# Sampling stage of a deformable bottleneck: transposes dealt three at a time, one table load and two DVE/ACT orders moved

## The chip, the cores and the metric

The kernel runs on one core of one Trainium2 chip. The metric is device time in microseconds (us), as the median of several runs. A core has five instruction queues that run side by side and meet at semaphores: TensorE (PE, matrix multiplies and transposes into PSUM), VectorE (DVE), ScalarE (ACT, activations and copies), GpSimd (POOL) and SyncE (SP, which issues the DMAs here). Each queue works through its own program in order.

## The reference

Two bottleneck blocks follow each other on x of 4 images x 256 channels x 16 x 16. The first is a deformable convolution block, the second a convolution block with quantised weights and activations:

```
out = relu(group_norm(conv1x1(x, w1)))                  # 256 -> 64 channels
om  = conv3x3(out, w_off) + b_off                       # 27 channels: x and y offsets, mask of 9 taps
sampled = bilinear_sample(out, grid_y + off_y, grid_x + off_x) * sigmoid(mask)
out = einsum('bckhw,ock->bohw', sampled, w2)            # 9 taps
out = relu(group_norm(out))
out = relu(group_norm(conv1x1(out, w3)) + x)            # 64 -> 256 channels
# second block: quantise -> conv1x1 -> depthwise 3x3 -> bn, relu -> conv3x3 -> bn, relu -> conv1x1 -> bn -> + residual, relu
```

## The kernel before, in words

The four images are held as `HALVES` = 2 by `B2` = 2. The change lies in the sampling stage, which does the bilinear sampling as matrix products. For each tile t (b2 = t // 2, and t % 2 is one half of the image's 256 output pixels) and half h there is one **unit** i = 2t + h, eight in all.

- **Hats.** DVE takes the differences of positions and coordinates (`differences`, L849), makes them into hat functions, and `apply_mask` (L863) multiplies one of the two by the mask. For tiles 2 and 3 ACT does the hat part (`distance`, L653, two activations).
- **g rows.** `make_g` (L874) on DVE is the product of the two hats, one 16 x 16 image of weights per output pixel and tap, into one of three buffers `g_rows`. Units 0 to 5 are made whole; the last two units (6 and 7) are made in thirds of three taps. `make_g` of unit i waits until the turns of unit i - 3 are done.
- **Turns.** `turn(n)` (L433) on PE transposes a third of a unit (12 PE transposes) into one of three PSUM slots. It waits for the unit's g rows and for the copy of turn n - 3, which frees its slot. There are 24 turns (n = 0 to 23). Turns 18 to 23 are, in this order, thirds of units 6, 7, 6, 7, 6, 7.
- **Copies.** `copy_g(n)` (L686) on ACT moves the slot of turn n to SBUF (`g_cols`). Between copies ACT does other work that is placed by n: `distance`, Sign, Abs and Identity of the second block's weights, and `root` and `normalise` of the second group norm of b2 = 0.
- **Samples.** `sample(t, a, b)` (L453) on PE multiplies taps a to b of tile t with the features (`v_sb`) and adds into `acc[b2]`; 4 matmuls a tap, of which the trace shows 8 records. It waits for the copies of the two turns that hold the tap.
- **Means.** `sample(1, 8, 8)` ends b2 = 0 and raises `sampled`; DVE's `moments(0)` then lets PE's `pair_sums(3, 0)` run, after which DVE's `pair_var`, ACT's `root(3, 0)` (behind copy 18), DVE's `pair_scale` and ACT's `normalise` (behind copy 19) make `feat2` for `conv3(0)` (L497), which starts the next stage. `conv3(0)` waits for `feat2` and for all 24 copies.

The order of turns and samples on PE is written out by hand (L466 to L494). `idle(n, bank)` (L336) are n matmuls on zeros that compute nothing. Ahead of the stage, ACT copies `v_sb` out of PSUM (`copy_v`, L663), the last of them at L681, and then loads the table of Sqrt (L696) before `copy_g(0)`; the table of Sigmoid was loaded at L670 for the masks.

Of the kernel before, what the change touches and what calls it, by code (L numbers as in the profile page):

```python
# [51 lines left out]
ROWS_Q = H // NQ  # L52
PER_SLOT = 3
SLOT_OF = (1, 2, 0)
IDLE_FIRST = 2
TURNS = TAPS // PER_SLOT

TAPS_A = 5
# [6 lines left out]
WHOLE = UNITS - HALVES  # L65
# [26 lines left out]
ACT = mybir.ActivationFunctionType  # L92
# [20 lines left out]
def build(nc, x, first, pairs, consts, woff, grid, w2, w3, wq, out):  # L113
    with ExitStack() as ctx:
# [6 lines left out]
        def sem(name):  # L121
            return ctx.enter_context(nc.semaphore(name))
# [116 lines left out]
        diff_ready = sem("diff_ready")  # L239
# [9 lines left out]
        sampled = sem("sampled")  # L249
# [85 lines left out]
        def _(pe):  # L335
# [97 lines left out]
            def turn(n):  # L433

                i, j = THIRDS[n]
                pe.wait_ge(g_ready, products_before(i, j))
                if n < TURNS:

                    pe.wait_ge(v_ready, (1, 6, 2 * T + 1)[n])
                else:  # L440

                    pe.wait_ge(g_copied, n - TURNS + 1)
                for k in range(PER_SLOT * j, PER_SLOT * j + PER_SLOT):
                    for q in range(NQ):
                        at = CB * (NQ * (k - PER_SLOT * j) + q)
                        for r in range(HALVES):
                            mm = nc.tensor.transpose(  # L447
                                slot[SLOT_OF[n % TURNS]][:, BANK * r + at:BANK * r + at + CB],
                                g_rows[i % 3][rows(r), k, ROWS_Q * q:ROWS_Q * q + ROWS_Q, :],
                                ident[rows(r), CB * r:CB * r + CB])  # L450
                mm.then_inc(turned, 1)

            def sample(t, first_tap, last_tap):  # L453

                b2, at = t // NQ, P * (t % NQ)
                for k in range(first_tap, last_tap + 1):
                    pe.wait_ge(g_copied, third_after(t, k))
                    for q in range(NQ):
                        for h in range(HALVES):
                            mm = nc.tensor.matmul(  # L460
                                acc[b2][rows(h), at:at + P], v_sb[:, B2 * h + b2, q, k, :],
                                g_cols[t][h][:, NQ * k + q, :],
                                start=(k == 0 and q == 0), stop=(k == TAPS - 1 and q == NQ - 1))
                return mm

            for n in range(2 * TURNS):  # L466
                turn(n)
            idle(IDLE_FIRST, acc[1][:])

            sample(0, 0, 2)  # L470
            for n, first_tap, last_tap in ((6, 3, 3), (7, 4, 4), (8, 5, 5), (9, 6, 6), (10, 7, 7), (11, 8, 8)):
                turn(n)
                sample(0, first_tap, last_tap)
            sample(1, 0, 2)
            for n, first_tap, last_tap in ((12, 3, 3), (13, 4, 4), (14, 5, 5), (15, 6, 6), (16, 7, 7)):
                turn(n)
                sample(1, first_tap, last_tap)
            turn(17)
            sample(1, 8, 8).then_inc(sampled, 1)
            sample(2, 0, 0)  # L480
            turn(18)
            sample(2, 1, 2)
            turn(19)
            pair_sums(3, 0)
            sample(2, 3, 3)
            turn(20)
            sample(2, 4, 5)
            turn(21)
            sample(2, 6, 6)
            turn(22)  # L490
            sample(2, 7, 7)
            turn(23)
            sample(2, 8, 8)
            sample(3, 0, 1)  # L494


# [116 lines left out]
        def _(a):  # L613
# [33 lines left out]
            def copy_omt(b2):  # L647
                a.wait_ge(omt_done, b2 + 1)
                nc.scalar.activation(omt_sb[:, b2].rearrange("p q h o -> p (q h o)"),
                                     slot[1][:, BANK * b2:BANK * b2 + NQ * CB], ACT.Copy).then_inc(omt_ready, 1)  # L650
                make_mask(b2)
# [21 lines left out]
            copy_v(0)  # L673
            copy_v(1)
            copy_omt(1)
            for i in range(2, 2 * T):
                copy_v(i)

            a.wait_ge(v_done, 2 * T + 1)
            for h in range(HALVES):  # L680
                last = nc.scalar.activation(v_sb[:, B2 * h:B2 * h + B2, :, V_MAIN, :],  # L681
                                            slot[0][:, BANK * h:BANK * h + T * CB].rearrange(
                                                "p (b q o) -> p b q o", b=B2, q=NQ), ACT.Copy)
# [9 lines left out]
                nc.scalar.activation(dst.rearrange("p k (r n) -> p k r n", r=HALVES),  # L693
                                     src.rearrange("p r (k n) -> p k r n", k=per), ACT.Copy).then_inc(g_copied, 1)

            nc.scalar.preload_act_table(ACT.Sqrt)  # L696
            for n in range(len(THIRDS)):
                copy_g(n)
                if n == 5:
                    distance(2)  # L700
                if n == 8:
                    a.wait_ge(wq_in, 16)
                    nc.scalar.activation(wq_sign[:], wq_sb[:], ACT.Sign).then_inc(sign_ready, 1)
                if n == 11:
                    distance(3)
                if n == 13:
                    nc.scalar.activation(wq_mag[:], wq_sb[:], ACT.Abs).then_inc(sign_ready, 1)
                if n == 16:
                    a.wait_ge(sign_ready, 2)
                    nc.scalar.activation(wq_mag[:], wq_mag[:], ACT.Identity, scale=SQRT2, bias=tiny_sb[:, 0:1]  # L710
                                         ).then_inc(sign_ready, 1)
                if n == 18:
                    root(3, 0)
                if n == 19:
                    normalise(3, 0, feat2[:, 0, :], acc[0][:, 0:N], feat2_ready)
# [64 lines left out]
            for i, (c, b2, h, n) in enumerate(PIECES):  # L780
                a.wait_ge(sum_ready, 4 * B2 + i + 1)
                if i == len(PIECES) - 1:
                    n = 1
# [4 lines left out]
        def _(dve):  # L788
# [23 lines left out]
            def moments(b2):  # L812

                settle(nc.vector.bn_stats(stats[:, b2, 0, :], acc[b2][:, 0:N]))  # L814
                nc.vector.bn_aggr(mv[:, b2, 0, :], stats[:, b2, 0, :]).then_inc(mv_ready, 1)

            def pair_var(done, b2):

                dve.wait_ge(sums_done, done)
                sums = sums_of(done, b2)  # L820
                ts(var[:, b2, 0:1], sums[:, 4:5], sums[:, 4:5], sums[:, 1:2], ALU.mult, ALU.add  # L821
                   ).then_inc(var_ready, 1)
# [26 lines left out]
            def differences(t):  # L849

                dve.wait_ge(omt_ready, t // NQ + 1)
                return tt(hats[:, t].rearrange("p h a k y -> p h (a k) y"),
                          omt_sb[:, t // NQ, t % NQ, :, 0:2 * TAPS].unsqueeze(3).to_broadcast(
                              [P, HALVES, 2 * TAPS, H]),
                          coord.unsqueeze(1).unsqueeze(1).to_broadcast([P, HALVES, 2 * TAPS, H]), ALU.subtract)
# [7 lines left out]
            def apply_mask(t):  # L863

                if t < NQ:
                    dve.wait_ge(hats_made, t + 1)
                else:
                    dve.wait_ge(relu1_ready, t - 1)
                dve.wait_ge(mask_ready, t // NQ + 1)
                tt(hats[:, t, :, 1], hats[:, t, :, 1],  # L870
                   mask[:, t // NQ, t % NQ].unsqueeze(3).to_broadcast([P, HALVES, TAPS, H]), ALU.mult
                   ).then_inc(hats_ready, 1)

            def make_g(i, first_tap=0, last_tap=TAPS - 1):  # L874

                t, h = i // HALVES, i % HALVES
                taps = slice(first_tap, last_tap + 1)
                shape = [P, last_tap + 1 - first_tap, H, W]
                dve.wait_ge(hats_ready, t + 1)
                if i >= 3:  # L880

                    dve.wait_ge(turned, TURNS * (i - 2))
                tt(g_rows[i % 3][:, taps], hats[:, t, h, 1, taps].unsqueeze(3).to_broadcast(shape),  # L883
                   hats[:, t, h, 0, taps].unsqueeze(2).to_broadcast(shape), ALU.mult).then_inc(g_ready, 1)
# [23 lines left out]
            settle(differences(1))  # L908
            make_hats(1)
            apply_mask(1)  # L910
            differences(2).then_inc(diff_ready, 1)
            make_g(2)
            make_g(3)
            apply_mask(2)
            differences(3).then_inc(diff_ready, 1)
            make_g(4)
            make_g(5)
            apply_mask(3)
            for j in range(TURNS):
                for i in (WHOLE, WHOLE + 1):  # L920
                    make_g(i, PER_SLOT * j, PER_SLOT * j + PER_SLOT - 1)
                if j == 0:
                    dve.wait_ge(sampled, 1)
                    moments(0)
                if j == 1:
                    pair_var(3, 0)
                    pair_scale(3, 0, V_GN2S, V_GN2B)

            def eight_moments(b2):
                for c in range(CH):  # L930
# [79 lines left out]
            last = residual(1)  # L1010
# [178 lines left out]
```

## Time and profile before

| | us |
|---|---|
| median of 3 runs | 99.76 (99.13 to 100.64) |
| profiled execution, device time | 99.62 |
| its span (first to last instruction) | 97.8 |
| PE busy / DVE busy / ACT busy | 80.4 / 66.7 / 54.4 |
| start of the span to the first sample | 27.4 |
| first sample to `conv3(0)` | 25.8 |
| `conv3(0)` to the end | 44.6 |

The profile is of one execution. Times inside it are us from the start of the span. A busy engine is not always the one that sets the end: the chain of work that ended last names, at each moment, the instruction that the end was waiting for. "PEclk" is the granted clock of TensorE, as a share of 2.4 GHz.

### The profile page before, as it was taken

To read this page: it belongs to the slowest core of one execution; us is meant where nothing else is said; L and a number is where in the kernel's file an instruction comes from. 1 tells how busy PE (TensorE), PEld (TensorE's weight loads), DVE (VectorE), ACT (ScalarE), POOL (GpSimd) and SP (SyncE) were. 2 spreads that over 40 slices of the span, in tenths; PEclk is the share of its full clock that TensorE was granted. 3 is DMA by queue.
4 is the path that set the end of the run, shared out by engine and by line. 5 is a ranking of instruction groups with operands and counts; after the bars stand their busy time and mean duration, and the time that the engine had idled before them with its cause. 6 is when DMAs were issued, how large, how long until landed. Compare 5 with 4: busy or idle time off the path is not lost.

```text
span 97.8 us, 2194 instructions
## 1 busy us (share of the span) xinstructions
PE 80.4 (82%) x891; PEld 55.1 (56%) x896; DVE 66.7 (68%) x184; ACT 54.4 (56%) x94; POOL 5.0 (5%) x10
## 2 busy tenths in 40 slices
PE   5989998973899999999999997999576949597400
PEld 1335654663678798788878884475132448283100
DVE  1235389999999935309693706595989785857960
ACT  5102566699976897996683005531638064444770
POOL 7401100000000000000004000000000000000000
PEclk9999999999579999999999999999999999999955
DMA  2999500000000000000000000000000000000066
GB/s 34 290 358 314 221 0 0 7 0 0 0 7 0 0 7 0 7 7 0 0 7 0 0 0 7 0 0 0 0 0 0 0 0 0 0 10 0 0 204 225
DMA packets 3274, 4.17 MB, mean 43 GB/s; under 512 B 256, under 2 KB 2688, under 8 KB 3264
## 3 DMA queue, kind: packets, MB, share of 16 engines
q1 hardware_dynamic: 2992, 3.76, 12.0%
q10 hardware_dynamic: 272, 0.26, 0.8%
q8 instruction: 7, 0.11, 0.5%
q14 instruction: 3, 0.02, 0.1%
HBM read 2.98 MB, written 1.05 MB: 41 GB/s over the span
## 4 chain that ended last, share of the span: by engine, by line
PE 56%; DVE 18%; ACT 12%; DMA 5%; issue 3%; SPq 2%; DVEq 0%; ACTq 0%
PE acc L460 19%; PE slot L447 12%; DMA x_sb<-x 5%; PE acc L590 5%; PE slot L501 4%; ACT v_sb L666 3%; DVE g_cols L1015 3%; ACT g_cols L785 3%; PE slot L375 2%; PE acc L339 2%; PE slot L339 2%; ACT pad L754 2%; DVE g_cols L969 1%; DVE unused L987 1%; PE slot L530 1%
## 5 line engine op out<-in xcount | busy, mean ns | idle before, releaser
L883 DVE TENSOR_TENSOR g_rows<-hats 128x2304 f32<-128x2304 f32 (+1 forms) x12 | 20.6, 1752 | 1.1 <-PE slot L447 1.0
L460 PE MATMUL acc<-g_cols,v_sb 128*64 128x128 f32 x288 | 21.0, 284 | 0.0
L693 ACT ACTIVATE g_cols<-slot 128x768 f32<-128x768 f32 x24 | 18.7, 814 | 3.4 <-PE slot L447 3.4
L460 PEld LDWEIGHTS acc<-g_cols,v_sb 128*64 128x64 f32 x288 | 15.7, 139 | 2.4 <-ACT g_cols L693 0.8
L447 PE MATMUL slot<-consts_sb,g_rows 64*128 64x64 f32 x288 | 14.5, 237 | 2.4 <-ACT g_cols L693 1.5
L339 PE MATMUL slot<-zeros 128*128 128x512 bf16 x49 | 14.0, 415 | 1.5 <-DVE zeros L804 1.2
L447 PEld LDWEIGHTS slot<-consts_sb,g_rows 64*128 64x128 f32 x288 | 11.6, 146 | 5.8 <-issue 4.8
L339 PEld LDWEIGHTS slot<-zeros 128*128 128x128 bf16 x53 | 5.2, 107 | 6.8 <-issue 2.5
L754 ACT ACTIVATE pad<-g_cols 64x256 bf16<-64x256 int8 x8 | 3.3, 418 | 4.8 <-DVE g_cols L1015 4.7
L814 DVE BATCH_NORM_STATS2 stats<-acc 128x6 f32<-128x256 f32 x4 | 1.7, 429 | 4.9 <-PE acc L460 2.9
L623 ACT ACTIVATE std<-var,eps_sb 128x1 f32<-128x1 f32 x4 | 1.2, 294 | 6.7 <-DVE var L821 6.7
L375 PE MATMUL slot<-feat,woff_sb 128*64 128x256 f32 x36 | 4.7, 385 | 0.0
L737 ACT ACTIVATE dev_sb<-slot 128x4 f32<-128x4 f32 x2 | 0.3, 174 | 7.5 <-PE slot L511 7.5
L933 DVE BATCH_NORM_STATS2 stats<-slot 128x6 f32<-128x256 f32 x8 | 3.0, 414 | 2.0 <-PE slot L501 2.0
L339 PE MATMUL acc<-zeros 128*128 128x512 bf16 x14 | 3.9, 396 | 0.3 <-issue 0.3
L501 PE MATMUL slot<-feat,w_sb 128*128 128x256 f32 x16 | 4.0, 392 | 0.1
L530 PE MATMUL slot<-consts_sb,mx 128*128 128x128 f32 x12 | 2.4, 282 | 1.8 <-DVE mx L973 1.8
L725 ACT ACTIVATE g_cols<-slot,gn_bias,gn_scale 128x256 f32<-128x256 f32 x6 | 2.9, 560 | 1.4 <-DVE gn_bias L951 1.4
L777 ACT ACTIVATE act<-raw,bn_off 128x256 f32<-128x256 f32 x4 | 2.0, 508 | 2.8 <-DVE mx L1091 2.8
L501 PEld LDWEIGHTS slot<-feat,w_sb 128*128 128x128 f32 x16 | 2.9, 189 | 1.1 <-ACT feat L628 0.6
L870 DVE TENSOR_TENSOR hats<-hats,mask 128x288 f32<-128x288 f32 x4 | 1.8, 452 | 2.4 <-ACT hats L659 2.4
L375 PEld LDWEIGHTS slot<-feat,woff_sb 128*64 128x64 f32 x36 | 2.7, 135 | 1.2
(128 smaller groups left out, 120.8 us busy)
## 6 DMA issues: line engine op xcount, KB each, us to landing
out<-g_cols SPq DMA_DIRECT2D x4, 256.0 KB, 2.3
x_sb<-x SPq DMA_DIRECT2D x3, 256.0 KB, 4.5
wq_sb<-wq SPq DMA_DIRECT2D x1, 484.5 KB, 6.3
woff_sb<-woff SPq DMA_DIRECT2D x1, 288.0 KB, 5.5
w_sb<-w SPq DMA_DIRECT2D x1, 288.0 KB, 5.6
x_sb<-x ACTq DMA_DIRECT2D x1, 256.0 KB, 3.0
w_sb<-w SPq DMA_DIRECT2D x1, 256.0 KB, 6.5
consts_sb<-consts SPq DMA_DIRECT2D x1, 232.0 KB, 5.4
```

What stands on the lines that cost most here:

```text
L339: nc.tensor.matmul(bank, zeros[:, 0:P], zeros[:], start=True, stop=True)
L375: mm = nc.tensor.matmul(slot[0][CB * p:CB * p + CB, BANK * b2:BANK * b2 + N], woff_sb[:, k, :], window(feat, b2, k), start=(s == 0), stop= ...
L447: mm = nc.tensor.transpose(slot[SLOT_OF[n % TURNS]][:, BANK * r + at:BANK * r + at + CB], g_rows[i % 3][rows(r), k, ROWS_Q * q:ROWS_Q * q ...
L460: mm = nc.tensor.matmul(acc[b2][rows(h), at:at + P], v_sb[:, B2 * h + b2, q, k, :], g_cols[t][h][:, NQ * k + q, :], start=(k == 0 and q == ...
L501: mm = nc.tensor.matmul(slot[c][:, BANK * b2 + N * h:BANK * b2 + N * h + N], w3_sb[:, h, P * c:P * c + P], feat2[:, b2, :], start=True, st ...
L530: nc.tensor.matmul(small[b2][:, P:2 * P], mx[:, n, b2:b2 + 1].to_broadcast([P, P]), ident, start=not biased, stop=True, is_transpose=not b ...
L590: mm = nc.tensor.matmul(acc[b2][rows(h), 0:N], weights(k), window(pad[:, b2], h, k), start=(k == 0), stop=(k == TAPS - 1))
L666: nc.scalar.activation(v_sb[:, B2 * h + b2, q, 0:V_MAIN, :].rearrange("p k o -> p (k o)"), v_banks[i % 4], ACT.Copy).then_inc(v_ready, 1)
L693: nc.scalar.activation(dst.rearrange("p k (r n) -> p k r n", r=HALVES), src.rearrange("p r (k n) -> p k r n", k=per), ACT.Copy).then_inc(g ...
L754: nc.scalar.activation(dst, src, ACT.Copy, scale=256.0).then_inc(hi_ready, 1)
L883: tt(g_rows[i % 3][:, taps], hats[:, t, h, 1, taps].unsqueeze(3).to_broadcast(shape), hats[:, t, h, 0, taps].unsqueeze(2).to_broadcast(sha ...
L933: last = nc.vector.bn_stats(stats[:, b2, HALVES * c + h, :], slot[c][:, BANK * b2 + N * h:BANK * b2 + N * h + N])
```

## The change

On PE, turns are dealt three at a time (a whole unit, or three thirds of units 6 and 7) between runs of two to six taps, instead of one turn between runs of mostly one tap. The dummy matmuls ahead of the first sample go from 2 to 3. On ACT, the load of Sqrt's table moves from behind the `v_sb` copies to behind the second mask; `distance(3)` moves from behind copy 11 to behind copy 8 and Sign from behind copy 8 to behind copy 10. On DVE, the differences of tile 2 come behind `make_g(2)` instead of ahead of it, those of tile 3 ahead of `apply_mask(2)`, and the last thirds move around the moments and the variance.

```
-IDLE_FIRST = 2
+IDLE_FIRST = 3
...
+            turns(0, 5)
             idle(IDLE_FIRST, acc[1][:])
-
-            sample(0, 0, 2)
-            for n, first_tap, last_tap in ((6, 3, 3), (7, 4, 4), (8, 5, 5), (9, 6, 6), (10, 7, 7), (11, 8, 8)):
-                turn(n)
-                sample(0, first_tap, last_tap)
...
+            sample(0, 0, 4)
+            turns(6, 8)
+            sample(0, 5, 6)
+            turns(9, 11)
+            sample(0, 7, 8)
+            sample(1, 0, 3)
+            turns(12, 14)
+            sample(1, 4, 6)
+            turns(15, 17)
+            sample(1, 7, 8).then_inc(sampled, 1)
+            sample(2, 0, 3)
+            turns(18, 20)
             pair_sums(3, 0)
...
+            sample(2, 4, 6)
+            turns(21, 23)
+            sample(2, 7, 8)
             sample(3, 0, 1)
...
             copy_omt(1)
+            nc.scalar.preload_act_table(ACT.Sqrt)
             for i in range(2, 2 * T):
                 copy_v(i)
...
-            nc.scalar.preload_act_table(ACT.Sqrt)
             for n in range(len(THIRDS)):
                 copy_g(n)
                 if n == 5:
                     distance(2)
-                if n == 8:
+                if n == 10:
                     a.wait_ge(wq_in, 16)
                     nc.scalar.activation(wq_sign[:], wq_sb[:], ACT.Sign).then_inc(sign_ready, 1)
-                if n == 11:
+                if n == 8:
                     distance(3)
...
+            make_g(2)
             differences(2).then_inc(diff_ready, 1)
-            make_g(2)
             make_g(3)
+            differences(3).then_inc(diff_ready, 1)
             apply_mask(2)
-            differences(3).then_inc(diff_ready, 1)
             make_g(4)
             make_g(5)
             apply_mask(3)
...
+            make_third(0, 0)
+            make_third(0, 1)
+            make_third(1, 0)
+            dve.wait_ge(sampled, 1)
+            moments(0)
+            make_third(1, 1)
+            make_third(2, 0)
+            pair_var(3, 0)
+            pair_scale(3, 0, V_GN2S, V_GN2B)
+            make_third(2, 1)
```

`turns(a, b)` calls `turn` for n = a to b. `make_third(j, h)` makes the third j of unit 6 + h. Before, the order was (0,0), (0,1), moments, (1,0), (1,1), variance and scale, (2,0), (2,1).

On PE, from the first sample on, L447 are the transposes of the turns (12 a turn) and L460 the matmuls of the samples (4 a tap). The rows of the kernel before:

```order
L447 MATMUL slot<-consts_sb,g_rows 128x64 x72
L339 MATMUL acc<-zeros 128x512 x2
L460 MATMUL acc<-g_cols,v_sb 64x128 x12
L447 MATMUL slot<-consts_sb,g_rows 128x64 x12
L460 MATMUL acc<-g_cols,v_sb 64x128 x4
L447 MATMUL slot<-consts_sb,g_rows 128x64 x12
L460 MATMUL acc<-g_cols,v_sb 64x128 x4
```

The rows of the changed kernel at the same place:

```order
L447 MATMUL slot<-consts_sb,g_rows 128x64 x72
L339 MATMUL acc<-zeros 128x512 x3
L460 MATMUL acc<-g_cols,v_sb 64x128 x20
L447 MATMUL slot<-consts_sb,g_rows 128x64 x36
L460 MATMUL acc<-g_cols,v_sb 64x128 x8
L447 MATMUL slot<-consts_sb,g_rows 128x64 x36
L460 MATMUL acc<-g_cols,v_sb 64x128 x24
```

Three taps and a turn, then one tap and a turn, have become five taps and three turns, then two taps and three turns, then six taps.

On ACT, around the table load, before:

```order
L644 ACTIVATE mask<-omt_sb 128x36
L666 ACTIVATE v_sb<-acc 128x512 x2
L666 ACTIVATE v_sb<-slot 128x512 x2
L666 ACTIVATE v_sb<-acc 128x512 x2
L681 ACTIVATE v_sb<-slot 128x4x64 x2
L696 ACT_TABLE_LOAD
L693 ACTIVATE g_cols<-slot 128x768 x6
```

And in the changed kernel (its lines are up to six smaller):

```order
L638 ACTIVATE mask<-omt_sb 128x36
L670 ACT_TABLE_LOAD
L660 ACTIVATE v_sb<-acc 128x512 x2
L660 ACTIVATE v_sb<-slot 128x512 x2
L660 ACTIVATE v_sb<-acc 128x512 x2
L676 ACTIVATE v_sb<-slot 128x4x64 x2
L688 ACTIVATE g_cols<-slot 128x768 x6
```

The load now stands between the mask and the third of the `v_sb` copies, and the first copy of a turn follows the last `v_sb` copy directly.

## Rows read from the trace of the kernel before

**Rows 1.** The page: busy time of PE, and its granted clock in 40 slices.

```profile
PE 80.4 (82%) x891; PEld 55.1 (56%) x896; DVE 66.7 (68%) x184; ACT 54.4 (56%) x94; POOL 5.0 (5%) x10
...
PEclk9999999999579999999999999999999999999955
```

**Rows 2.** The chain that ended last: start us, us, what (x counts records).

```profile
27.41 1.86 PE acc L460 x24
29.27 0.52 PE slot L447 x12
29.79 0.59 PE acc L460 x8
...
35.32 1.90 PE acc L460 x32
...
44.82 1.02 PE acc L460 x16
...
46.37 0.31 PE acc L357 x2
46.68 0.22 PE acc L358 x2
...
51.77 1.46 PE acc L460 x24
53.23 1.93 PE slot L501 x8
...
65.86 1.08 PE acc L339 x5
```

**Rows 3.** Two windows: busy us by engine, then granted clock, DMA share, GB/s.

```profile
24.80:28.20 3.40, 3.03 (x33) 2.44 (x36) 3.40 (x2) 3.37 (x6) 0.00 (x0) 0.50 0.00 0
28.20:53.20 25.00, 25.00 (x449) 20.52 (x445) 16.67 (x22) 19.38 (x26) 0.82 (x1) 1.00 0.01 3
```

**Rows 4.** Timeline of ACT, 14.5 to 28 us: start, us, what, idle before it.

```profile
17.09 0.23 ACT L644 ACTIVATE mask<-omt_sb 128x36 f32<-128x36 f32 x1
18.06 1.09 ACT L666 ACTIVATE v_sb<-acc 128x512 f32<-128x512 f32 x2 [0.73 <-PE acc L413]
...
21.20 0.67 ACT L681 ACTIVATE v_sb<-slot 128x256 f32<-128x256 f32 x2
21.88 1.28 ACT L696 ACT_TABLE_LOAD   x1
23.18 4.32 ACT L693 ACTIVATE g_cols<-slot 128x768 f32<-128x768 f32 x6
27.33 0.73 ACT L657 ACTIVATE hats<-hats 128x576 f32<-128x576 f32 x1
```

**Rows 5.** Timeline of PE, 14.5 to 30 us, the turns and dummies ahead of the samples.

```profile
22.01 0.59 PE L447 MATMUL slot<-consts_sb,g_rows 64*128 64x64 f32 x12 [0.71 <-ACT v_sb L681]
24.13 2.31 PE L447 MATMUL slot<-consts_sb,g_rows 64*128 64x64 f32 x36 [1.53 <-ACT g_cols L693]
26.77 0.63 PE L339 MATMUL acc<-zeros 128*128 128x512 bf16 x1 [0.33 <-issue]
29.20 0.59 PE L447 MATMUL slot<-consts_sb,g_rows 64*128 64x64 f32 x12
```

**Rows 6.** Timeline of PE, 20.2 to 24 us: two turns in a row at full clock.

```profile
20.32 0.98 PE L447 MATMUL slot<-consts_sb,g_rows 64*128 64x64 f32 x22
```

**Rows 7.** Timeline of ACT, 28 to 62 us: copies and what lies between them.

```profile
28.09 0.77 ACT L659 ACTIVATE hats<-hats,one_sb 128x576 f32<-128x576 f32 x1
29.82 0.81 ACT L693 ACTIVATE g_cols<-slot 128x768 f32<-128x768 f32 x1 [0.96 <-PE slot L447]
...
32.75 1.00 ACT L703 ACTIVATE wq_sign<-wq_sb 128x969 f32<-128x969 f32 x1
...
47.26 0.29 ACT L623 ACTIVATE std<-var,eps_sb 128x1 f32<-128x1 f32 x1 [1.59 <-DVE var L821]
48.16 0.56 ACT L628 ACTIVATE feat<-acc,gn_bias,gn_scale 128x256 f32<-128x256 f32 x1
```

**Rows 8.** Timeline of DVE, 37 to 50 us: moments, variance, last thirds.

```profile
43.91 0.43 DVE L814 BATCH_NORM_STATS2 stats<-acc 128x6 f32<-128x256 f32 x1 [2.88 <-PE acc L460]
...
46.94 0.29 DVE L821 TENSOR_SCALAR var<-acc 128x1 f32<-128x1 f32 x1 [0.66 <-PE acc L358]
...
48.00 1.82 DVE L883 TENSOR_TENSOR g_rows<-hats 128x768 f32<-128x768 f32 x2
```

More of the change, by code:

```diff
@@ L464, in sample, with turns @@
                 return mm
-            for n in range(2 * TURNS):
-                turn(n)
+            def turns(first, last):
+                for n in range(first, last + 1):
+                    turn(n)
+            turns(0, 5)
             idle(IDLE_FIRST, acc[1][:])
-            sample(0, 0, 2)
-            for n, first_tap, last_tap in ((6, 3, 3), (7, 4, 4), (8, 5, 5), (9, 6, 6), (10, 7, 7), (11, 8, 8)):
-                turn(n)
-                sample(0, first_tap, last_tap)
[L474 to L483, printed above, removed]
-            pair_sums(3, 0)
[L485 to L493, printed above, removed]
+            sample(0, 0, 4)
[10 more added lines that the diff above has]
+            turns(18, 20)
+            pair_sums(3, 0)
+            sample(2, 4, 6)
+            turns(21, 23)
+            sample(2, 7, 8)
             sample(3, 0, 1)
@@ L918, in _, with make_third @@
             apply_mask(3)
[L919 to L927, printed above, removed]
+            def make_third(j, h):
+                make_g(WHOLE + h, PER_SLOT * j, PER_SLOT * j + PER_SLOT - 1)
+            make_third(0, 0)
[8 more added lines that the diff above has]
+            make_third(2, 1)
             def eight_moments(b2):
```

## The prediction

> **What bounds the kernel now.** I read four views in this order. The page first: PE is busy 80.4 of 97.8 us, and its clock row shows full speed everywhere but in one dip near the eleventh slice and at the very end [rows 1]. Then the chain that ended last, because a busy share says nothing about who is waited for: from 27.41 to 53.23 us the chain is PE alone, a turn of 0.52 us, a tap of 0.59 us, and so on, with no gap [rows 2]. The window 28.20 to 53.20 agrees: PE busy 25.00 of 25.00 us, ACT 19.38, DVE 16.67, clock 1.00 [rows 3]. So in the sampling stage time comes off only where PE's own stream gets shorter, and an engine may not be slowed past its slack, 5.6 us for ACT. Last, the timelines ahead of it: there PE waits for ACT. It waited 0.71 us for the last v_sb copy and 1.53 us for copy 0 [rows 5], and copy 0 stood behind the table load of 1.28 us [rows 4].
>
> **What a change of block costs on PE.** Runs of taps in the chain: one tap 0.59, two 1.02, three 1.46, four 1.90 us [rows 2]. Each further tap is 0.435 us, so 0.155 us of every run is paid once, whatever its length. A lone turn is 0.52 us. Turns in a row at full clock show only ahead of the stage: 22 transposes in 0.98 us, of which the last takes about 0.22 us from start to end (a lone turn is 0.59 us with that end and 12 transposes, [rows 5]); 0.76 us over 21 steps is 0.036 us, 0.43 us a turn [rows 6]. That is my price for a turn inside a group, and 0.52 for the last of a group. The bounds: 0.52 (nothing saved), and about 0.40 if the row still holds some waiting. I take 0.43, since the row shows it.
>
> **The sum, part by part.**
>
> *Table load.* Before: the last v_sb copy ends at 21.87, the load and its gaps take 1.31 us, copy 0 starts at 23.18 [rows 4]. After: the load follows the mask, which ended at 17.32. ACT was idle there until 18.06, so 0.73 us of the load are covered by ACT's wait for PE, and the rest, 17.32 + 1.31 - 18.06 = 0.57 us, pushes all remaining v_sb copies, which are back to back. Copy 0 comes 1.31 - 0.57 = 0.74 us earlier. Turns 3 to 5 wait for copies 0 to 2, so they come 0.74 us earlier as well. PE's v_sb matmuls wait for these copies through their four banks; they had finished at 20.3, ahead of ACT, and 0.6 us of delay there is hidden.
>
> *Third dummy bank.* Five dummies in a row at full clock took 1.08 us [rows 2], 0.216 each; at half clock, which is granted from 24.8 to 28.2 us [rows 3], twice that, 0.43 us. If the clock does what it did, the first sample starts at 27.41 - 0.74 + 0.43 = 27.10 us. Then the clock is half for another 1.1 us, which costs 0.55 us. The five taps of the first run end at 27.10 + 0.155 + 5 x 0.435 + 0.55 = 29.98 us. (The same sum for before, 27.41 + 1.46 + 0.4, gives 29.27, where turn 6 stands.)
>
> *From turn 6 to conv3(0).* Before: 29.27 to 53.23 us, 23.96 us. In it are 18 turns (9.36 us at 0.52), 18 runs with 26 taps (18 x 0.155 + 26 x 0.435 = 14.10 us) and the pair sums (0.53 us): 23.99 us, so the prices close. After: 18 turns in 6 groups, 6 x (2 x 0.43 + 0.52) = 8.28 us; 6 runs with 24 taps, 6 x 0.155 + 24 x 0.435 = 11.37 us; pair sums 0.53. Sum 20.18 us, without waits.
>
> *Waits that the groups make.* A copy starts 0.62 us after its turn starts (29.20 to 29.82), takes 0.81, and six in a row take 4.32, so 0.70 each [rows 4, 5, 7]. PE follows a copy's end by about 0.14 us (copy 0 ends 23.99, turn 3 starts 24.13). The turns of a group come 0.43 apart and the copies 0.70, so ACT falls behind in each group and catches up in the taps. I walked through the six groups with turn 6 at 0:
> - Copies 6 to 8 start at 0.62, 1.32, 2.02. distance(3), 1.45 us [rows 4, 7], now stands behind copy 8, so copy 9 runs 4.17 to 4.98. PE reaches tap (1,0), which needs it, at 1.38 + 1.02 + 1.38 + 1.02 = 4.80: a wait of 0.3 us.
> - Copy 14 stands behind Abs (0.9 us, as Sign, [rows 7]) and turn 17 needs it: 0.15 us.
> - Copy 19 stands behind root(3, 0) and copy 20 behind normalise. The variance now comes behind two more thirds, but these (0.91 us each, [rows 8]) finish while PE does turns 18 to 20 and the pair sums. Sums ready, DVE 0.3, ACT 0.3, copy 19, normalise 0.45, copy 20: turn 23 comes about 0.3 us late.
> Together 0.75 us. Distance(3) earlier and the new DVE orders are at nothing in the sum: unit 3 is due on PE about 2.8 us after turn 6 and DVE has it before 30 us, and DVE then waits for PE as it did (2.88 us idle ahead of the moments, [rows 8]).
>
> conv3(0) starts at 29.98 + 20.18 + 0.75 = 50.9 us against 53.23: 2.3 us. With turns at 0.40 it would be 2.8. I take 2.5 us. What follows conv3(0) is untouched, and DVE's weight work moves up with the thirds. The profiled execution would be 99.62 - 2.5 = 97.1 us; it lies 0.14 under the median, so against 99.76 the forecast is **97.3 us**.
>
> **The table load, row and rule.** The row is 1.28 us, and copy 0 starts 0.02 us after its end [rows 4]. The Trainium skill (ScalarE: Activation LUTs, What ACT_TABLE_LOAD costs) says that a switch costs a load of about 1283 ns and then a drain of about 1380 ns, 2.66 us. The trace agrees with the load and shows no drain.
>
> **The rivals.**
>
> *B. The clock does not fall.* Before, the clock was full while PE did turns 0 to 3 and waited between 21.1 and 24.1 us, and half from 24.8 [rows 3, 5]. After, the wait ahead of copy 0's turn is 0.74 us shorter, and three banks follow. If it holds, turn 5 (0.27), three dummies (0.65) and the taps (0.55) are done at full speed: 1.5 us more, 95.8 us. Against it: PE still does nothing but a few turns from 20.3 to 24.8.
>
> *C. Less from the groups.* If turns in a row cost 0.52 us like lone ones (12 x 0.09 = 1.1 us), or if each of six groups waits 0.3 us for copies (1.8 instead of 0.75): 98.3 us.
>
> *D. The order does nothing,* since ACT takes the bound: only the table load is left, less the dummy, about 99.3 us. ACT's 18 copies at 0.70 and 4.9 us of other work are 17.5 us in a stretch of 21; this speaks against it.
>
> *E. A second pause at the load's new place.* If after the load ACT stood still once more for as long, 1.29 us, nothing there would hide it, since 0.73 us of cover are used up: 98.6 us. All v_sb copies and copy 0 would be late. The skill's drain, above, would act like this. The row on the old place speaks against it.
>
> *F. Slower: the clock falls inside the sampling.* Each 3.4 us stretch at half clock in dense work costs some 1.5 us (as in B). Two more give 100.3, three more 101.8 us, more than 2% slower; from two on the change has lost. Mechanism: transposes that come three turns at a time, 1.38 us, do not keep the clock up as samples do. Before, turns were 9.4 of 24.0 us and the clock stayed at 1.00 [rows 3]; after, 8.3 of 20.9, the same share, only in longer pieces. The Trainium skill (TensorE: Matmul & The Clock Gate, Part 4) says that transposes do not count as busy for the clock; by that page the dip at 24.8, behind turns alone, would be no accident, and the trace agrees so far.
>
> **How the numbers follow.** A, the forecast (97.3, own range 96.7 to 98.0): 48 in 100. B 25, C 14, D 4, E 3, F 6 (4 of them over 2% slower). About 2% is what a measurement of this kernel tells from no change, that is under 97.8 or over 101.8 us. Faster: three quarters of A, B, a little of C: 0.62. Slower: 0.04. The rest, 0.34, within 2%. The range reaches to B below and C and E above: 95.5 to 98.9; it leaves out D, F and the edge of B.
>
> **What would show it.** Taps in runs of 2 to 6 at 0.155 + 0.435 each, and a group of three turns in 1.38 us (1.56 would be C). Copy 0 at 22.4 to 22.5 us and the load directly behind the mask with no idle time behind it (else E). PE idle time in front of tap (1,0), turn 17 and turn 23 of 0.3, 0.15 and 0.3 us. The clock row with one dip in the eleventh slice (none is B, more is F). conv3(0) at 50.7 to 50.9 us. I am wrong if PE waits for copies in every group, or if the clock falls at another place.

## The result

| | before | changed |
|---|---|---|
| median | 100.16 us (4 runs, 99.13 to 100.64) | 96.16 us (4 runs, 96.05 to 96.38) |
| ratio | | 0.963, 95% interval 0.957 to 0.969 |
| profiled execution, span | 97.8 us | 94.2 us |

The change makes the kernel 4.0 us faster (one more run of before moved its median from 99.76 to 100.16). Medians here are of all runs; the ratios leave out runs more than 1.5% above the fastest run of their kernel. I forecast 97.3 us, a gain of 2.5 us, and gave a quarter of the chance to rival B (the clock does not fall, 95.8 us). B is what happened. All lines below carry the changed kernel's numbers: L447 and L460 are still turns and samples, L688 is `copy_g`, L670 the table load, L495 `conv3`.

The page of the changed kernel, its clock row against [rows 1]:

```profile
span 94.2 us, 2201 instructions
...
PE 78.2 (83%) x897; PEld 54.1 (57%) x897; DVE 66.4 (70%) x184; ACT 53.3 (57%) x94; POOL 5.0 (5%) x10
...
PEclk9999999999999999999999999999999999999985
```

The dip in the eleventh slice is gone. The timeline of ACT (start, us, what, idle before), against [rows 4]:

```profile
17.51 0.23 ACT L638 ACTIVATE mask<-omt_sb 128x36 f32<-128x36 f32 x1
17.76 1.28 ACT L670 ACT_TABLE_LOAD   x1
19.05 1.08 ACT L660 ACTIVATE v_sb<-acc 128x512 f32<-128x512 f32 x2
20.02 1.09 ACT L660 ACTIVATE v_sb<-slot 128x512 f32<-128x512 f32 x2
20.98 1.12 ACT L660 ACTIVATE v_sb<-acc 128x512 f32<-128x512 f32 x2
21.93 0.72 ACT L676 ACTIVATE v_sb<-slot 128x256 f32<-128x256 f32 x2
22.46 4.41 ACT L688 ACTIVATE g_cols<-slot 128x768 f32<-128x768 f32 x6
```

The load stands directly behind the mask, and the next copy starts 0.01 us after it: no second pause (rival E). Behind the load each pair of v_sb copies starts 0.96 us after the last; before it was 1.08 us. PE's v_sb matmuls, which those copies wait for, came 1.08 us a pair apart too (timelines of PE and ACT before):

```profile
16.95 1.13 PE L413 MATMUL acc<-w_sb,feat_flat 64*128 64x512 f32 x4
18.03 1.13 PE L413 MATMUL slot<-w_sb,feat_flat 64*128 64x512 f32 x4
...
19.14 1.08 ACT L666 ACTIVATE v_sb<-slot 128x512 f32<-128x512 f32 x2
```

The timeline of PE, against [rows 2] and [rows 5]:

```profile
22.80 2.70 PE L447 MATMUL slot<-consts_sb,g_rows 64*128 64x64 f32 x48 [0.50 <-ACT v_sb L676]
25.43 0.82 PE L339 MATMUL acc<-zeros 128*128 128x512 bf16 x3
26.18 2.40 PE L460 MATMUL acc<-g_cols,v_sb 128*64 128x128 f32 x40
28.51 1.34 PE L447 MATMUL slot<-consts_sb,g_rows 64*128 64x64 f32 x36
29.78 1.09 PE L460 MATMUL acc<-g_cols,v_sb 128*64 128x128 f32 x16
30.81 1.34 PE L447 MATMUL slot<-consts_sb,g_rows 64*128 64x64 f32 x36
32.08 1.09 PE L460 MATMUL acc<-g_cols,v_sb 128*64 128x128 f32 x16
33.49 1.97 PE L460 MATMUL acc<-g_cols,v_sb 128*64 128x128 f32 x32 [0.31 <-ACT g_cols L688]
...
38.12 0.96 PE L447 MATMUL slot<-consts_sb,g_rows 64*128 64x64 f32 x24
39.27 0.59 PE L447 MATMUL slot<-consts_sb,g_rows 64*128 64x64 f32 x12 [0.19 <-ACT g_cols L688]
...
45.83 0.96 PE L447 MATMUL slot<-consts_sb,g_rows 64*128 64x64 f32 x24
47.09 0.59 PE L447 MATMUL slot<-consts_sb,g_rows 64*128 64x64 f32 x12 [0.30 <-ACT g_cols L688]
47.61 1.97 PE L460 MATMUL acc<-g_cols,v_sb 128*64 128x128 f32 x32
49.51 1.99 PE L495 MATMUL slot<-feat,w_sb 128*128 128x256 f32 x8
```

A group of three turns takes 1.27 us (28.51 to 29.78), so with 0.52 for its last a turn inside costs 0.375 us. PE waits at the three places that were forecast. Tap (1,0) comes at 33.49, 1.41 us after a run of two taps (1.03) began: 0.38 us. Turn 17 comes 1.15 us after turn 15 and turn 23 1.26 us after turn 21, where two turns need 0.75: 0.40 and 0.51 us. (The bracket names less, since it counts from the modelled end of the matmul ahead.)

Spans can't be subtracted as they are. The first v_sb matmul (L413) starts anywhere from 14.40 to 15.37 us in the fourteen traces, although nothing ahead of it was changed. One reason shows at the span's start: dummies follow each other there every 0.43 us at first and every 0.22 us later, and PE's clock becomes full after 4.3 to 6.6 us, at another moment in each execution (the clock row doesn't show this). Another is a wait for the input's DMA (0.57 us in a_oldtab_warm, the latest). So I measure from that matmul, 14.61 us in before and 15.03 us in the changed kernel, up to `conv3(0)`. Each value below is the difference of two starts in the timeline of PE:

| us | to first sample | then to turn 6 | then to conv3(0) | together | median of runs |
|---|---|---|---|---|---|
| before | 12.72 | 1.86 (3 taps) | 23.96 | 38.55 | 100.2 to 100.5 |
| changed | 11.15 | 2.34 (5 taps) | 21.00 | 34.48 | 96.16 |

The sum is 4.07 us less, the medians 4.0. What follows `conv3(0)` did not change (44.67 and 44.66 us).

### The profile page after: what moved, and what is told of

It reads as the page before. It is cut to its first block, busy times and chain, and to the rows that moved or that the text cites. A ratio compares the mean times of both kernels' runs of the same rounds, so it can differ in the third digit from the quotient of the medians.

```text
span 94.2 us, 2201 instructions
## 1 busy us (share of the span) xinstructions
PE 78.2 (83%) x897; PEld 54.1 (57%) x897; DVE 66.4 (70%) x184; ACT 53.3 (57%) x94; POOL 5.0 (5%) x10
## 3 DMA queue, kind: packets, MB, share of 16 engines
HBM read 2.98 MB, written 1.05 MB: 43 GB/s over the span
## 4 chain that ended last, share of the span: by engine, by line
PE 54%; ACT 22%; DVE 17%; issue 3%; DVEq 0%; ACTq 0%
PE acc L460 13%; ACT g_cols L688 7%; PE slot L447 6%; PE slot L339 5%; PE slot L375 5%; PE acc L584 5%; ACT v_sb L660 4%; PE slot L495 4%; PE acc L350 3%; DVE g_cols L1014 3%; PE acc L339 2%; ACT g_cols L779 2%; ACT pad L748 2%; DVE g_cols L1105 2%; DVE g_cols L968 2%
## 5 line engine op out<-in xcount | busy, mean ns | idle before, releaser
L688 ACT ACTIVATE g_cols<-slot 128x768 f32<-128x768 f32 x24 | 18.0, 841 | 1.6 <-PE slot L447 1.6
L460 PE MATMUL acc<-g_cols,v_sb 128*64 128x128 f32 x288 | 18.2, 276 | 0.3 <-ACT g_cols L688 0.3
L460 PEld LDWEIGHTS acc<-g_cols,v_sb 128*64 128x64 f32 x288 | 15.5, 137 | 1.7 <-ACT g_cols L688 1.0
L339 PE MATMUL slot<-zeros 128*128 128x512 bf16 x53 | 14.7, 413 | 1.2 <-DVE zeros L798 1.2
L447 PE MATMUL slot<-consts_sb,g_rows 64*128 64x64 f32 x288 | 12.2, 227 | 1.3 <-ACT v_sb L676 0.5
L447 PEld LDWEIGHTS slot<-consts_sb,g_rows 64*128 64x128 f32 x288 | 10.5, 139 | 3.0 <-issue 2.4
L495 PE MATMUL slot<-feat,w_sb 128*128 128x256 f32 x16 | 4.0, 392 | 0.1
L495 PEld LDWEIGHTS slot<-feat,w_sb 128*128 128x128 f32 x16 | 2.9, 189 | 1.1 <-ACT feat L622 0.6
L584 PE MATMUL acc<-pad,pegq 128*64 128x256 bf16 x36 | 2.3, 277 | 1.2 <-ACT pad L748 1.2
```

The lines of the kernel that those rows point to most:

```text
L339: nc.tensor.matmul(bank, zeros[:, 0:P], zeros[:], start=True, stop=True)
L447: mm = nc.tensor.transpose(slot[SLOT_OF[n % TURNS]][:, BANK * r + at:BANK * r + at + CB], g_rows[i % 3][rows(r), k, ROWS_Q * q:ROWS_Q * q ...
L460: mm = nc.tensor.matmul(acc[b2][rows(h), at:at + P], v_sb[:, B2 * h + b2, q, k, :], g_cols[t][h][:, NQ * k + q, :], start=(k == 0 and q == ...
L495: mm = nc.tensor.matmul(slot[c][:, BANK * b2 + N * h:BANK * b2 + N * h + N], w3_sb[:, h, P * c:P * c + P], feat2[:, b2, :], start=True, st ...
L584: mm = nc.tensor.matmul(acc[b2][rows(h), 0:N], weights(k), window(pad[:, b2], h, k), start=(k == 0), stop=(k == TAPS - 1))
```

## The experiments

**Is the surplus the clock?** b_warm is before, with five dummies in PE's wait for copy 0:

```
             for n in range(2 * TURNS):
                 turn(n)
+                if n == 2:
+                    idle(5, acc[1][:])
```

> The kernel before with five dummy matmuls (5 x 0.216 us) put behind turn 2, into the 1.7 us in which TensorE waits for copy 0. They fit into the wait at full clock, so no engine's real work moves. Theory CLOCK (the half-clock stretch ahead of the first samples is set off by the empty wait and costs about 1.5 us, and the change's surplus over my 2.5 us was that it went away): the window 24.8 to 28.2 is granted full clock, 1.2 to 1.6 us less than the kernel before, about 98.5. Rival PHASE (the dip comes and goes by chance or has another cause): dip as before, time within 0.3 us of the kernel before.

Measured: 99.07 us, ratio to before 0.989 (0.981 to 0.996). b_warm's clock row and PE's timeline:

```profile
PEclk9999999999999999999999999999999999999995
...
23.05 1.03 PE L339 MATMUL acc<-zeros 128*128 128x512 bf16 x4 [0.16 <-issue]
24.43 2.00 PE L447 MATMUL slot<-consts_sb,g_rows 64*128 64x64 f32 x36 [0.35 <-ACT g_cols L695]
26.36 0.60 PE L339 MATMUL acc<-zeros 128*128 128x512 bf16 x2
26.89 1.53 PE L460 MATMUL acc<-g_cols,v_sb 128*64 128x128 f32 x24
```

The dip is gone, and 1.14 us with it: 11.98 us to the first sample for 12.72, 1.46 for three taps for 1.86, and the same 23.96 behind them. The mean granted clock was 0.986 to 0.990 in its four runs, and 0.947 to 0.974 in all 21 runs of before taken beside the experiments, so the dip belongs to before, and not to one profile. (The mean also holds the half clock at the end of every kernel, 1.8 to 4.8 us long: the profiles without a dip have 0.974 to 0.990, the two with one 0.958 and 0.971. A single run near 0.973 proves neither.) Work that computes nothing, put where PE stood still, made the kernel faster. Theory CLOCK holds; PHASE falls as the cause of these 1.14 us. That the wait alone sets off the dip is not shown (b_order, below).

**The table load alone.** b_table:

```
             copy_omt(1)
+            nc.scalar.preload_act_table(ACT.Sqrt)
...
-            nc.scalar.preload_act_table(ACT.Sqrt)
             for n in range(len(THIRDS)):
```

> The kernel before with only the table load moved behind the second mask. Load hidden for 0.73 of 1.31 us: copy 0 about 0.74 us earlier, and the time 0.6 to 0.8 us less if the clock falls as before. If the shorter wait alone is enough to hold the clock: 2.0 to 2.3 us less.

Measured: 97.75 us, ratio 0.976 (0.970 to 0.982), 2.7 us less; in the trace 2.2 us (10.94 to the first sample, 1.46, 23.95). The dip is gone with the load alone. Of the 2.2 us, 1.14 are the clock as in b_warm; 1.04 us are left for the load (b_warm's 11.98 less 10.94), not the 0.74 of the forecast.

**The order alone.** b_order has only PE's new order, with two dummies and everything else as before. Its diff is PE's part of the change.

> The kernel before with only TensorE's order changed to groups of three turns and runs of two to six taps (two dummies, old ACT and DVE orders, old table load). By the traces: twelve fewer runs of taps (12 x 0.155 = 1.9 us) and twelve turns that follow a turn (12 x 0.14 = 1.7 us by the changed kernel's groups of 1.27 us), less waits for copies of 1.0 to 1.4 us: 2.0 to 2.6 us less than before with the clock falling as before. If the groups were worth nothing without the other parts: within 0.3 us of before.

Measured: 98.30 us, the median of 96.89 us at a granted clock of 0.983, and 97.58, 99.02 and 99.06 us at 0.970 to 0.973. The ratio to before is 0.970 (0.960 to 0.980) for the first two alone, and 0.979 for the medians of all runs (98.30 and 100.43). PE waits 1.53 us for copy 0 here as in before. By the mean clocks the granted clock fell in most of the runs and not in all; only the fastest was profiled, and it had no dip: 11.98, 2.33 (five taps) and 20.92 us. So the order takes 23.96 + 1.46 - 2.33 - 20.92 = 2.17 us at full clock.

**The order taken away.** a_oldorder is the changed kernel with PE's old order, all else as changed.

> The changed kernel with TensorE's old order (one turn between runs of mostly one tap), all else as changed: three dummies, table load behind the mask, new ACT and DVE orders. The clock should hold, as in the changed kernel, so this is the price of the order alone. By the traces: 1.9 us for twelve runs of taps, 1.7 us for twelve turns, less the 1.4 us that the changed kernel waits for copies in its groups: 2.2 us more than the changed kernel, about 98.3. If the order were worth little once the clock holds: under 97.

Measured: 98.22 us, 2.1 us over the changed kernel; trace 11.16, 1.46, 23.94, together 36.56 for 34.48. It agrees with b_order.

**The table load put back.** a_oldtab is the changed kernel with b_table's edit the other way round.

> The changed kernel with the table load back behind the v_sb copies. 0.74 us more than the changed kernel (about 96.9) if the clock holds, 2.2 us more (about 98.4) if the longer wait for copy 0 makes the clock fall again in the stretch before the samples.

Measured: 98.83 us, the median of 97.21 us at a clock of 0.983, and 98.74, 98.92 and 99.52 us at 0.971, 0.973 and 0.956. The profile, of the run of 98.74, has a dip:

```profile
PEclk9999999999958999999999999999999999999995
...
24.61 2.08 PE L447 MATMUL slot<-consts_sb,g_rows 64*128 64x64 f32 x36 [1.53 <-ACT g_cols L687]
27.02 1.06 PE L339 MATMUL acc<-zeros 128*128 128x512 bf16 x2 [0.33 <-issue]
28.01 2.17 PE L460 MATMUL acc<-g_cols,v_sb 128*64 128x128 f32 x20
```

Here the half clock (26.4 to 29.8 us) lies later than in before and reaches 1.8 us into the five taps (the view ended at 30 us and shows 20 of their 40 records; turn 6 starts at 31.19): 12.92 us to the first sample, and 3.19 for the taps instead of 2.34. The wait of 1.53 us is back, and with it a time that moves by 2.3 us from one execution to the next. The one run at a clock of 0.983 is 1.05 us over the changed kernel.

**And put back with the wait filled.** a_oldtab_warm is a_oldtab with b_warm's five dummies behind turn 2.

> The changed kernel with the table load back behind the v_sb copies, and five dummies behind turn 2 to fill TensorE's wait for copy 0. Theory CLOCK: no half-clock stretch before the end, and the 0.74 us of the later copy 0 are all that is left of the 2.7 us that the old place cost: 96.7 to 97.1. Rival (the load's place costs more than its uncovered time by another way, the clock is a bystander): 98 or more, as without the dummies.

Measured: 97.31 us (96.59 to 97.62). The trace has no dip: 12.21, 2.34, 21.00, together 35.55. That is 1.07 us over the changed kernel; in time 1.15. (No run but the profiled one is known to be without a dip; the mean clocks are 0.973 to 0.990.) So the old place of the load costs 1.07 us in itself, and the rest of a_oldtab's 2.7 us is the clock. My 0.74 us was missed here too: the rival that the clock is a bystander falls, and the load's own price is nearly half as large again as I said.

**The ACT and DVE orders.** a_oldboth is the changed kernel with the old orders on both (the end of the cut is the last thirds, as in before):

```
-                if n == 10:
+                if n == 8:
                     a.wait_ge(wq_in, 16)
...
-                if n == 8:
+                if n == 11:
                     distance(3)
...
             apply_mask(1)
-            make_g(2)
             differences(2).then_inc(diff_ready, 1)
+            make_g(2)
             make_g(3)
-            differences(3).then_inc(diff_ready, 1)
             apply_mask(2)
+            differences(3).then_inc(diff_ready, 1)
...
```

> The changed kernel with the old orders on ACT (Sign behind copy 8, distance(3) behind copy 11) and on DVE (differences, last thirds). My prediction put these moves at nothing. Walking the groups through with the old orders gives 0.1 to 0.4 us more; within 0.3 us of the changed kernel if they are worth nothing, over 1 us more if the last thirds come too late for turns 18 to 20.

Measured: 95.76 us (95.46 to 96.07), 0.4 us under the changed kernel by the medians; trace 11.15, 2.34, 20.92: 0.08 us less from turn 6 on. Together these moves gain nothing. Without the distance between copies 8 and 9, the wait for tap (1,0) is all but gone, but turn 17 waits longer, and turn 23 now waits for DVE. So ACT's part of the move costs and DVE's part gives back; neither was run by itself. PE's timeline of a_oldboth:

```profile
31.77 2.90 PE L460 MATMUL acc<-g_cols,v_sb 128*64 128x128 f32 x48
...
38.56 0.59 PE L447 MATMUL slot<-consts_sb,g_rows 64*128 64x64 f32 x12 [0.28 <-ACT g_cols L688]
...
46.70 0.59 PE L447 MATMUL slot<-consts_sb,g_rows 64*128 64x64 f32 x12 [0.28 <-DVE g_rows L877]
```

**Who makes the groups wait?** c_acts moves ACT's other work out of the way of the copies that a group needs:

```
-                if n == 10:
+                if n == 11:
                     a.wait_ge(wq_in, 16)
...
-                if n == 8:
+                if n == 10:
                     distance(3)
-                if n == 13:
+                if n == 14:
                     nc.scalar.activation(wq_mag[:], wq_sb[:], ACT.Abs).then_inc(sign_ready, 1)
-                if n == 16:
+                if n == 17:
                     a.wait_ge(sign_ready, 2)
...
-                if n == 18:
-                    root(3, 0)
                 if n == 19:
+                    root(3, 0)
+                if n == 20:
                     normalise(3, 0, feat2[:, 0, :], acc[0][:, 0:N], feat2_ready)
```

> The changed kernel with ACT's other work moved out of the way of the copies that groups wait for: distance(3) behind copy 10, Sign behind 11, Abs behind 14, Identity behind 17, root(3, 0) behind 19, normalise behind 20. The changed kernel's trace shows TensorE waiting in front of tap (1,0), turn 17 and turn 23, 1.3 us with the run price paid again. If ACT's other work is the cause, these go away for the most part and the time is 0.7 to 1.2 us under the changed kernel, about 95.2. If the copies' own pace (0.70 a copy against 0.38 a turn) is the cause, the waits stay and the time is within 0.3 us.

Measured: 94.70 us (94.13 to 94.70), ratio to before 0.946 (0.940 to 0.952). The trace has 11.15, 2.34 and 19.54 us: 1.46 us less from turn 6 on, more than the 0.7 to 1.2 that I expected, since the waits and the run paid anew go altogether. PE's timeline of c_acts:

```profile
32.25 2.84 PE L460 MATMUL acc<-g_cols,v_sb 128*64 128x128 f32 x48
35.02 1.34 PE L447 MATMUL slot<-consts_sb,g_rows 64*128 64x64 f32 x36
...
45.06 1.34 PE L447 MATMUL slot<-consts_sb,g_rows 64*128 64x64 f32 x36
46.34 1.97 PE L460 MATMUL acc<-g_cols,v_sb 128*64 128x128 f32 x32
48.23 1.99 PE L495 MATMUL slot<-feat,w_sb 128*128 128x256 f32 x8
```

No group waits. The copies' own pace of 0.70 us is not the cause; the other work between them is. The sum of the prices without waits, 6 x 1.27 + 6 x 0.155 + 24 x 0.435 + 0.53 = 19.52 us, meets the 19.54 of the trace.

**Are the dummies ahead of the samples needed?** c_idle1 and c_idle0 are c_acts with `IDLE_FIRST` = 1 and 0.

> c_acts with one dummy bank instead of three ahead of the first sample. The first sample waits for copy 3, which by c_acts' trace ends at about 25.6 us, while the three dummies end at 26.3: so the dummies hold it up by some 0.5 us. If the clock holds without them: 0.4 to 0.5 us under c_acts. If two dummies fewer let the clock fall in some runs: those are 1.5 us or more slower, and the median is at or above c_acts.

> c_acts with no dummy bank ahead of the first sample. The wait for copy 3 sets the first sample, so time as with one dummy (within 0.2 us) if the clock holds; if the clock needs the dummies, a half-clock stretch at the first samples and 1.5 us or more over c_acts.

Measured: 94.09 us (93.44 to 94.95) and 93.99 us (93.63 to 94.20). In the traces the first sample comes at 10.72 and 10.50 us for 11.15, and neither has a dip. So the dummies are not needed here once the wait ahead of turn 3 is gone; the third dummy only pushed the samples back. By time alone the two and c_acts can't be told apart with certainty; by the traces they save 0.43 and 0.51 us. (c_idle0 starts 0.65 us earlier and loses 0.15 us again behind turn 6.) c_idle0 is the fastest version by the median: ratio to before 0.941 (0.933 to 0.948).

**What a block pays for.** e_sw128 and e_sw64 put a tiny matmul of two columns behind the first and the second turn of the groups 6 to 8 up to 15 to 17:

```
             for n in range(first, last + 1):
                 turn(n)
+                if 6 <= first <= 15 and n < last:
+                    nc.tensor.matmul(acc[1][0:CB, 300:302], zeros[:, 0:CB], zeros[:, 0:2], start=True, stop=True)
```

That is e_sw128; e_sw64 has `acc[1][:, 300:302]`, `zeros[0:CB, 0:P]` and `zeros[0:CB, 0:2]`.

> The changed kernel with a tiny matmul (2 columns, bf16 zeros, into an unused corner of a bank) between the turns of the groups 6-8 to 15-17, eight of them, in the samples' form (all 128 rows, 64 columns of the array). Theory SHAPE (the price of a block is paid when PE goes between the turns' form, 64 rows, and the samples' form, 128 rows): each tiny matmul adds 0.25 to 0.30 us, the step from turn 6 to turn 7 goes from 0.38 to about 0.65 us. Rival START (what costs is the first wait or the start of any new run, whatever the form): about the same as its twin in the turns' form.

> The same eight tiny matmuls in the turns' form (64 rows, 128 columns of the array). Theory SHAPE: under 0.1 us each, the step from turn 6 to turn 7 at 0.40 to 0.47 us. Rival START: 0.25 us or more each, as its twin.

Measured, one run each: 97.28 and 96.08 us. The timelines of PE, first e_sw128, then e_sw64 (the column behind MATMUL's operands is the part of the array, rows by columns):

```profile
28.66 0.59 PE L447 MATMUL slot<-consts_sb,g_rows 64*128 64x64 f32 x12
29.18 0.19 PE L470 MATMUL acc<-zeros 128*64 128x2 bf16 x1
29.30 0.59 PE L447 MATMUL slot<-consts_sb,g_rows 64*128 64x64 f32 x12
```

```profile
28.61 0.59 PE L447 MATMUL slot<-consts_sb,g_rows 64*128 64x64 f32 x12
29.03 0.17 PE L470 MATMUL acc<-zeros 64*128 64x2 bf16 x1
29.04 0.60 PE L447 MATMUL slot<-consts_sb,g_rows 64*128 64x64 f32 x13
```

From turn 6 to turn 7 it is 0.64 us with the samples' form between, 0.43 with the turns' form, and 0.375 with nothing. The same two columns cost 0.265 us in the one form and 0.055 in the other. (Together the eight show as 1.2 us and not 2.1: from turn 6 to conv3(0) it is 22.16 us in e_sw128 and 21.00 in e_sw64 and in the changed kernel, as waits for copies shrink by part of what they cost.) So SHAPE holds for the larger part: the form alone makes 0.21 us of the 0.265. A round trip in the kernel is 0.155 us on the run and 0.52 - 0.375 = 0.14 us on the turn, 0.295 in all; what the last 0.085 us are, starting a run or something else, these two runs don't separate. Twelve fewer round trips are 3.5 us, less 1.4 us of waits that the groups bring: 2.1 us. The Trainium skill says (TensorEngine Tiling (Array Packing), Key Properties) that a change of the tiling mode drains TensorE, and not a mere change of tile. The prices in both runs agree; the drain itself shows in no row.

## Why the prediction was right and wrong

**What bounds the kernel: right.** PE was the chain, and the gain is PE's stream getting shorter. My sum gave a gain of 2.3 us, and I took 2.5 because turns at 0.40 us would give 2.8 (it is 2.7: 12 x 0.03 on top). Up to turn 6 the sum was some 1.8 us too long, 1.5 by the clock and 0.3 by the table load; behind turn 6 it was right by luck.

**The clock: wrong, and the largest part.** I took the half-clock stretch over from the trace of before, although the change touches just what stood ahead of it. b_warm shows that it cost 1.14 us, and b_table that the load's move alone ends it. I had priced it at 1.5 us in rival B, with three dummies and five taps under it; in before there are two and three. a_oldtab, which has as many as the changed kernel, paid 1.56 us. The forecast less one or the other is 95.7 to 96.2 us. This step, the clock taken as unchanged, is what the forecast had wrong. Against B I had argued that PE does little between 20.3 and 24.8 us. What differs is the longest empty piece: 1.53 us ahead of turn 3 before, 0.50 us ahead of turn 2 after, with turns 2 to 5 then 0.70 us apart, at the pace of the copies, as turns 3 to 5 were before. The wait is not the whole condition either: b_order's profile has the 1.53 us and no dip.

**The table load: right in kind, 0.74 us forecast, 1.05 to 1.07 measured.** The step that failed is "all remaining v_sb copies, which are back to back". They were not held by ACT but by PE's v_sb matmuls, which came every 0.54 us. With the load ahead of them, PE gets its matmuls done in the meantime, and the copies then run at their own 0.48 us: of the push of 0.57 us, 0.26 is caught up before the last pair (6.59 us after the first v_sb matmul before, 6.90 now). And the load's old place cost 1.45 us, not 1.31: copy 0 started 1.98 us behind the start of the last pair (21.20 to 23.18) and now 0.53 (21.93 to 22.46), since copies that follow each other overlap. Copy 0 ended up 1.14 us earlier (23.18 - 14.61 against 22.46 - 15.03), and turn 3 by 1.05.

**The third dummy: 0.22 us at full clock,** as priced, and not needed (c_idle1, c_idle0).

**From turn 6 to conv3(0): forecast 20.93 us, measured 21.00,** by two errors that cancel. A run of taps, 0.155 + 0.435 a tap, was exact. A turn inside a group costs 0.375 us, not 0.43: the row of 22 transposes at the start held the seam with the last v_sb matmuls. That is 12 x 0.055 = 0.66 us less. The waits, forecast at 0.75 us, are 0.38 + 0.40 + 0.51 = 1.29, and 0.155 more because tap (1,0) starts a run anew: faster turns only come sooner to copies that are no earlier. The places were right, all three, and so was the cause (c_acts).

**ACT and DVE orders at nothing: right in sum** (a_oldboth, 0.08 us), by two parts that cancel. **Rival C** had a group of turns at 1.56 us or a wait in each of six groups; the trace has 1.27 us and three waits, though these, at 1.29 us, lie midway between its 1.8 and my 0.75. **D** fell with b_order and a_oldorder, **E** with the timeline of ACT and a_oldtab_warm. **F** did not happen: turns in threes do not bring the clock down, the clock was 1.00 throughout the sampling in every trace of a kernel with groups once the wait ahead of turn 3 was filled or gone, with up to 36 transposes in a row. Whether transposes count for the clock at all is not decided by that.

The parts, from the traces, up to conv3(0): table load -1.05, third dummy +0.22, clock -1.14, order -2.09 (+0.87 for two more taps ahead of turn 6, -2.96 behind it), together -4.06 of 4.07 us.

## What to carry to other kernels

Where a change shortens a wait of TensorE, ask what the clock did behind that wait, and test it by filling the wait with dummies: it takes one line. Keep matmuls of one tiling form together, as long as the engine that empties PSUM has no other work between the copies that the next group needs. A chain of copies that looks back to back may be paced by the engine ahead of it; only then does a delay at its head come free.

## What was not expected of the hardware

- In before the granted clock was half for 3.4 us behind a stretch in which PE had waited 0.71 us ahead of one turn and 1.53 us ahead of the next. Five dummies of 0.21 us in the second wait kept it full, by the mean clocks in four of four runs. With the wait of 1.53 us but the new order (b_order), the clock fell by the mean clocks in some executions and not in others; why one and not the other is open. One thing differs in the three profiles with that wait empty: at the span's start the clock became full after 4.3 us in before and 5.9 in a_oldtab, which have the dip, and after 6.6 in b_order, which has none. Three profiles don't decide whether that matters.
- The price of a fall depends on where it lands: 1.14 us in before, and 1.56 us in a_oldtab (12.92 - 12.21 ahead of the first sample and 3.19 - 2.34 in the taps, against a_oldtab_warm, which differs in the five dummies alone).
- A switch of form and back, around a matmul of two columns, costs 0.265 us with that matmul, 0.6 of a whole tap (0.435 us); the same matmul without a switch costs 0.055.
